# Reordered opening and closing steps of a folded mixture-and-adapter kernel

## Chip, cores and metric

One NeuronCore of a Trainium2 chip runs the whole program as one launch. The metric is the device time of one execution in microseconds (us); lower is better. TensorE (PE) multiplies, VectorE (DVE) and ScalarE (ACT) do the elementwise work and read PSUM, GpSimd (POOL) does elementwise work in SBUF, and SyncE (SP) issues nearly all transfers.

## What is computed

The input x is 64 tiles of 128 rows by 1024 (128 samples of 64 channels). Two layers follow each other; cut to what matters:

```python
c   = einsum('bct,bcd->bdt', x, W[condition])           # channel mix, per sample
q   = c @ Wq.T;  scores = router(q)/sqrt(48) + log_rel  # 256 slots, top 8
w   = softmax over the top 8 of (q . keys)/8 + log_rel
aux = (w @ values) @ Wvd.T @ Wvu.T
u   = clip(0.5*log1p(var)/mean(log1p(var)) + 2.5*sigmoid(gelu(c@Wu1.T+bu1)@Wu2.T+bu2), 0, 5)
x   = x + c + gate(u) * aux
y   = x @ base_weight.T + base_bias + (x @ A[id].T) @ B[id].T   # low-rank adapter
x   = x + base(y) + 0.5 * inverse_fourier(decoded(y))
```

Everything after x in the second layer is linear, so the weights are folded into one 1024 x 1024 matrix M and the adapters into rows of two tables. The mean of log1p(var) runs over all rows, so all 64 tiles must have been seen once before the gate of the first can be computed.

## The kernel before

There are three stages. `setup_stage` and `fold_stage` (to about 276 us of the profiled execution) build M while the variance of every tile is taken. `main_stage` then splits M and small tables into high and low parts and runs the tiles.

M is not used as it is: seven half-size products per tile pair (blocks B11, T1, B21, T2, T3, T4, B22; the named sums T3, T4, B22 are formed on POOL by `t_sums`) give the product of two tiles. Every block is held as two 16-bit parts in two halves, so there are 14 units in the order of `UNITS` (B11, T2, B21, T3, T1, T4, B22). `m_high(u)` on ACT makes the high part (L1197), `m_low(u)` on DVE the low part (L1731). PE waits for a unit before its first use (`product_unit`, L1560).

The main stage is a software pipeline written out by hand as `step(n, q)` on each engine: steps 0 to 3, a loop over 56 steps, then steps 60 to 66. In step n, PE does for tile n the narrow product (8 chunks, L1634), the mix (L1684), and half of the seven products of a pair (an odd step `product_first`, an even one `product_second`); between its chunks stand, for tile n-1, the transposes and the small products of the gate (`aux`, `aux_t`, `adapter`); and for tile n-3 twelve matmuls (L1665 and L1676) that write the output into `out_ps`, from where ACT copies it (L1269) and SP stores it (L1072). Each engine executes its list in order, so a step's wait holds back all that stands behind it there. Order is set by these lists and by semaphores, nothing else.

What stands around the change, by line:

- Opening on DVE: L1780 to L1811, ending in the router's operand (L1803 to L1811, seven instructions that read `score_ps` and the keys and end in `router_split`). Behind it in step 0: the low part of the narrow product `pa_lo` (L1865), which PE needs for the mix; `wa_low`, `row_constants` (with two memsets, L1824); the query (L1892), `variance_norm` (L1830), m_low(2) and (3).
- Step 0 on PE: mix, a matmul for the mean over all rows into `score_ps` (L1692, which waits for `router_split`), the value operand (L1495, whose table `av_t` SP loads at L1103), transpose of the query, scores.
- Step 1 on PE: `aux_t` waits for `u_sb` of DVE (L1854, L1857), itself behind the gate's small steps (L1987 to L1993) and, in step 0, behind m_low(4) and m_low(5). On ACT `split_x(2, 2)` (L1282) and m_high(8) stand behind p1 (L1279); on DVE m_low(8) (L1943) stands before gelu (L1946), lsum (L1949) and u2 (L1957), for which PE waits before the T3 units.
- End of step 2: ACT copies V, the folded value matrix in `out_ps`, to `rhs_a` (L1344); DVE makes its low part twice (`v_low`, L1828, once for each slot of `rhs_b`), then raises `vb_ready`.
- SP before its loop: loads of tiles 4 and 5, then a wait for `vb_ready`, then the adapter rows of tiles 0 and 1 (`load_adapters`, L1117 to L1123).
- Tail: step 65 makes the output of tile 62 (slot 0 of `pm_hi`, `pm_lo`), step 66 that of tile 63 (slot 1), both in `out_ps`. In `last_quarter` the last sum of slot 0 (`u2`, L1849) is taken after the last product; slot 1 is complete before.

## Time and profile before

| | us |
|---|---|
| median of 3 runs (lowest to highest) | 1505.54 (1505.38 to 1508.84) |
| the profiled execution, own time | 1507.83 |
| its span, first to last instruction | 1505.8 |
| PE busy | 1447.3 (96%) |
| DVE busy | 970.4 (64%) |
| ACT busy | 882.6 (59%) |
| POOL busy | 695.1 (46%) |

The page of the profile gives the busy time of each engine, the span in 40 slices with the clock that TensorE was granted, the chain of work that ended last, and the costliest groups. The trace behind it can be asked for what each engine waited for, for the order of instructions in a stretch, and for the busy time by stretch. Lines (L86) are lines of the kernel; L86, L87 and L88 are the three matmuls of every split product.

### The profile page before, as it was taken

The page shows a single profiled execution, that of the slowest core. Times are in us where ns is not written, and L with a number is a line of the kernel's source. Part 1 is how long each engine was busy: PE and PEld are TensorE (multiplying, and loading weights), DVE is VectorE, ACT ScalarE, POOL GpSimd, SP SyncE. Part 2 cuts the span into 40 slices and gives each one's busy share as a digit, 9 for nine tenths or more (in the row PEclk, how much of TensorE's full clock was granted, in tenths as well). Part 3 has the DMA queues.
Part 4 walks back from the last instruction along what each step waited for, and adds up shares of the span by engine and source line. Part 5 has one row for each costly group of instructions (what it writes and reads, how often), then busy time and mean ns, then how long its engine had stood idle before and what let it go on. Part 6 is the DMA issues. An engine that isn't in the chain of part 4 may idle for free.

```text
span 1505.8 us, 28751 instructions
## 1 busy us (share of the span) xinstructions
PE 1447.3 (96%) x7300; PEld 904.2 (60%) x7300; DVE 970.4 (64%) x2744; ACT 882.6 (59%) x1841; POOL 695.1 (46%) x539
## 2 busy tenths in 40 slices
PE   6899999977899999999999999999999999999997
PEld 3677777553555656665555556666555555656664
DVE  6767888887466666666666666566666666666663
ACT  4667666645456555665566555566555556555652
POOL 4756666555444444444444444444444444444440
PEclk9999999979899999999999999999999999999999
DMA  9687665240333333333333333223333333333322
GB/s 309 228 276 257 195 186 171 75 108 5 102 95 93 103 99 100 101 101 95 93 93 96 101 105 92 92 92 92 92 99 103 95 93 93 101 101 99 110 59 77
DMA packets 160951, 176.14 MB, mean 117 GB/s; under 512 B 104851, under 2 KB 123238, under 8 KB 160785
## 3 DMA queue, kind: packets, MB, share of 16 engines
q1 hardware_dynamic: 156118, 161.56, 34.9%
q10 hardware_dynamic: 4795, 14.15, 2.8%
q8 instruction: 15, 0.25, 0.1%
q14 instruction: 23, 0.19, 0.0%
HBM read 135.97 MB, written 39.32 MB: 116 GB/s over the span
## 4 chain that ended last, share of the span: by engine, by line
PE 78%; POOL 7%; issue 6%; DVE 5%; SPq 2%; DMA 1%; ACT 1%; POOLq 0%; ACTq 0%; DVEq 0%
PE pair L86 20%; PE pair L88 19%; PE pair L87 19%; PE pair L1676 7%; POOL v_lo L256 6%; PE pair L1665 6%; PE pair L1507 2%; PE pair L1552 1%; PE pair L1546 1%; PE pair L1545 1%; DVE m_lo L1736 1%; DMA w_kinds<-w_kinds_sb 1%; PE pair L1526 1%; PE pair L1513 0%; SPq L351 0%
## 5 line engine op out<-in xcount | busy, mean ns | idle before, releaser
L1375 POOL TENSOR_TENSOR t_narrow<-t_a_raw,t_narrow 128x256 f16<-128x256 f32 x64 | 42.9, 671 | 574.6 <-ACT x_hi L1189 574.6
L86 PE MATMUL pair<-m_hi,s_hi 128*128 128x512 f16 x512 | 195.6, 382 | 7.8 <-DVE t_u L1957 5.4
L256 POOL TENSOR_TENSOR v_lo<-v_x,v_hi 128x1024 fp32r<-128x1024 f32 x64 | 156.1, 2442 | 91.5 <-ACT v_hi L250 91.4
L87 PE MATMUL pair<-m_lo,s_hi 128*128 128x512 f16 x512 | 194.6, 380 | 0.0
L88 PE MATMUL pair<-m_hi,s_lo 128*128 128x512 f16 x512 | 194.6, 380 | 0.0
L1398 POOL TENSOR_TENSOR s_lo<-t_xt,s_hi 128x512 f16<-128x512 f32 x128 | 145.4, 1166 | 60.6 <-ACT s_hi L1195 60.6
L86 PE MATMUL pair<-t_narrow,x_hi 128*128 128x352 f16 x512 | 161.3, 315 | 1.0 <-DVE t_narrow L1793 1.0
L87 PE MATMUL pair<-t_narrow,x_hi 128*128 128x352 f16 x512 | 161.1, 315 | 0.0
L88 PE MATMUL pair<-t_narrow,x_lo 128*128 128x352 f16 x512 | 161.0, 314 | 0.0
L1377 POOL TENSOR_TENSOR x_lo<-t_xt,x_hi 128x512 f16<-128x512 f32 x128 | 152.0, 1208 | 0.0
L86 PE MATMUL pair<-m_hi,x_hi 128*128 128x512 f16 x384 | 147.5, 384 | 0.3 <-DVE u L1916 0.3
L87 PE MATMUL pair<-m_lo,x_hi 128*128 128x512 f16 x384 | 146.6, 382 | 0.0
L88 PE MATMUL pair<-m_hi,x_lo 128*128 128x512 f16 x384 | 146.5, 382 | 0.0
L1865 DVE SCALAR_TENSOR_TENSOR t_pa_lo<-pair,t_unscale,t_pa_hi 128x320 fp32r<-128x320 f32 (+1 forms) x128 | 45.4, 396 | 121.4 <-ACT t_pa_hi L1256 121.4
L1909 DVE SCALAR_TENSOR_TENSOR t_arg<-t_z 128x256 f32<-128x256 f32 x64 | 58.1, 908 | 85.0 <-ACT t_z L1275 85.0
L247 ACT ACTIVATE squares<-v_x 128x1024 bf16<-128x1024 f32 x64 | 67.4, 1054 | 49.5 <-DVE blk_lo L807 32.7
L1251 ACT CAST t_lhs_a<-pair 128x128 fp32r<-128x128 f32 x64 | 17.0, 266 | 135.4 <-PE pair L1513 135.4
L1295 ACT ACTIVATE t_probs<-t_logits,t_col 128x256 f32<-128x256 f32 x64 | 32.4, 507 | 108.0 <-DVE t_col L1940 108.0
L86 PEld LDWEIGHTS pair<-m_hi,s_hi 128*128 128x128 f16 x512 | 50.0, 98 | 75.6 <-DVE t_u L1957 21.9
L88 PEld LDWEIGHTS pair<-m_hi,s_lo 128*128 128x128 f16 x512 | 50.2, 98 | 60.7 <-issue 0.6
L1185 ACT ACTIVATE t_xt<-t_xt,t_scale 128x512 f32<-128x512 f32 x128 | 84.9, 714 | 0.0
L1269 ACT COPY t_out_sb<-pair 128x1024 f32<-128x1024 f32 x64 | 64.6, 1009 | 28.7 <-PE pair L1676 28.7
(291 smaller groups left out, 3695.2 us busy)
## 6 DMA issues: line engine op xcount, KB each, us to landing
v_x<-in_x SPq DMA_DIRECT2D x64, 512.0 KB, 3.4
t_xt<-in_x_t SPq DMA_DIRECT2D x64, 512.0 KB, 3.2
out<-t_out_sb SPq DMA_DIRECT2D x64, 512.0 KB, 2.7
rhs_b<-bk_hi SPq DMA_DIRECT2D x256, 64.0 KB, 2.3
t_a_raw<-in_lora_a SPq DMA_DIRECT2D x128, 64.0 KB, 2.8
t_bd<-w_kinds SPq DMA_DIRECT2D x128, 64.0 KB, 2.2
t_rhs_c<-bk_lo SPq DMA_DIRECT2D x128, 64.0 KB, 2.2
blk_raw<-in_left_blocks ACTq DMA_DIRECT2D x10, 512.0 KB, 4.7
```

Source lines behind the costliest of these rows:

```text
L86: pe.matmul(out, a_hi, b_hi, start=start, stop=False, skip_group_check=skip)
L87: pe.matmul(out, a_hi, b_lo, start=False, stop=False, skip_group_check=skip)
L88: return pe.matmul(out, a_lo, b_hi, start=False, stop=stop, skip_group_check=skip)
L247: act.activation(v["squares"][:, s, :], v["v_x"][:, slot, :], ACT.Square, accum_out=g["x_sq"][:, bass.ds(n, 1)])
L256: pool.tensor_tensor(v["v_lo"][:, s, :], v["v_x"][:, slot, :], f(v["v_hi"][:, s, :]), ALU.subtract).then_inc(v["v_lo_ready"], 1)
L1185: last = act.activation(rows, rows, ACT.Identity, scale=x_scale(i, half))
L1269: act.copy(b["out_sb"][:, o, :], out_ps[:]).then_inc(s["out_ready"], 1)
L1377: last = pool.tensor_tensor(x16[q][1][:, cols], b["xt"][:, p, cols], x16[q][0][:, cols], ALU.subtract)
L1398: last = pool.tensor_tensor(s16[q // 2][1][:, slot, cols], b["xt"][:, slot, cols], s16[q // 2][0][:, slot, cols], ALU.subtract)
L1665: pe.matmul(out_ps[:, c], lhs, rhs[o][:, c], start=begin, stop=False)
L1676: last = pe.matmul(out_ps[:, c], lhs, rhs[:, c], start=False, stop=end)
L1909: dve.scalar_tensor_tensor(b["arg"][:], b["z2"][:], 1.0, b["z"][:], ALU.add, ALU.mult).then_inc(s["arg_ready"], 1)
```

## The change

It touches no loop iteration; all of it is in the opening steps 0 to 3 and the last two steps.

1. DVE, opening: the constant row's low part (L1784) goes behind the low parts of Wu and Wq; the two memsets go ahead of `a_low(3)`; the router's operand becomes `router_low()` and goes behind z in step 0. The mean's matmul writes the product's bank `pm_ps` and waits for `const_placed`, not for `router_split`.
2. M's low parts on DVE: m_low(5) from the end of step 0 to behind `pa_lo` of step 1; 6 behind z, 7 behind u2, 8 behind the gate of step 1.
3. ACT: an early one-element Tanh in step 0; `sums_high(0, 0)` behind z2 of step 0; the gate's Tanh ahead of e_t in step 0; `split_x(2, 2)` ahead of the query's copy in step 1.
4. V: ACT's copy behind tanh of step 2 (with waits for M's unit and POOL's sum), one `v_low` behind m_low(13), the second slot by a DVE copy in step 3 behind `pa_lo`; PE waits for it before the units of step 3.
5. SP: the adapter rows of tiles 0 and 1 wait for M's low parts, not for V, and go ahead of the loads of tiles 4 and 5.
6. Tail: step 65 makes tile 63, step 66 tile 62, the latter in `pair[2]`; ACT copies its left half, DVE its right half; SP stores in that order.
7. Three SBUF tiles change places.

```diff
-        def store(j, p):
+        def store(j, p, ready=None):
             off = sp.snap(j * (P * HID)) if not isinstance(j, int) else j * P * HID
-            ready = sp.snap(j + 1) if not isinstance(j, int) else j + 1
+            if ready is None:
+                ready = sp.snap(j + 1) if not isinstance(j, int) else j + 1
             sp.wait_ge(s["out_ready"], ready)
             sp.dma_start(bass.AP(t["out"].tensor, off, [[HID, P], [1, HID]]), b["out_sb"][:, p, :]
...
-        load_x(5, 1)
-        sp.wait_ge(s["vb_ready"], 1)
+        sp.wait_ge(s["m16_lo_ready"], len(UNITS))
         sp.wait_ge(s["const_cleared"], 1)
         sp.wait_ge(f_["bk_stored"], 32 * LBLK)
         load_adapters(0, 0)
         load_adapters(1, 1)
+        load_x(4, 0)
+        load_x(5, 1)
...
+            if isinstance(n, int) and n == NT + 3:
+                sp.wait_ge(s["half_ready"], 1)
+            if isinstance(n, int) and n > NT + 1:
+                store(old_tile(n - 1), 1 - p, n - 3)
+            else:
+                store(n - 4, p)
...
+
+    def old_tile(n):
+
+        return 2 * NT - n if isinstance(n, int) and n > NT else n - 3
+
+    def old_slot(n, q):
+        return old_tile(n) % 2 if isinstance(n, int) else 1 - q % 2
+
+    def last_one(n):
+        return isinstance(n, int) and n == NT + 2
...
-            o = 1 - p
+            o = old_slot(n, q)
...
+                act.activation(col[0:1, 15:16], g["ones"][0:1, 0:1], ACT.Tanh)
+            if isinstance(n, int) and n == 1:
+                act.wait_ge(s["wa_stored"], 16)
+            if p == 1 and (not isinstance(n, int) or n + 2 < NT):
                 split_x(n + 1, (q + 1) % 4)
...
             if has_old(n):
                 act.wait_ge(s["out_done"], n - 2)
-                act.wait_ge(moved[o], arrived(n - 3, o, 16))
-                act.copy(b["out_sb"][:, o, :], out_ps[:]).then_inc(s["out_ready"], 1)
+                act.wait_ge(moved[o], arrived(old_tile(n), o, 16))
+                if last_one(n):
+                    act.copy(b["out_sb"][:, o, LEFT], pair[2][:, LEFT]).then_inc(s["out_ready"], 1)
+                else:
+                    act.copy(b["out_sb"][:, o, :], out_ps[:]).then_inc(s["out_ready"], 1)
...
+            if isinstance(n, int) and n == 0:
+                act.wait_ge(s["wa_mm_done"], KC // 2)
+                sums_high(0, 0)
...
             if isinstance(n, int) and n == 1:
-                act.wait_ge(s["wa_stored"], 16)
-                split_x(2, 2)
...
+            if isinstance(n, int) and n == 2:
+                act.wait_ge(s["m16_lo_ready"], m_units(T1, 2))
+                act.wait_ge(s["t_ready"], 2 * SUMMED.index(B22) + 2)
+                act.wait_ge(s["v_mm_ready"], 2)
+                act.copy(b["rhs_a"][:], out_ps[:]).then_inc(s["va_ready"], 1)
...
+            start = isinstance(n, int) and n == 0
+            if start:
+                gate_tanh()
             if has_new(n):
                 act.wait_ge(s["et_done"], n + 1)
                 act.copy(b["e_t"][:].rearrange("p c n -> p (c n)"), misc_ps[:, P:3 * P]
                          ).then_inc(s["et_ready"], 1)
-                act.wait_ge(s["unorm_ready"], n + 1)
-                act.activation(c1(GTANH), c1(UNORM), ACT.Tanh, scale=b["gates"][:, 4:5],
-                               bias=b["gates"][:, 5:6]).then_inc(s["gtanh_ready"], 1)
+            if has_new(n) and not start:
+                gate_tanh()
...
-                act.wait_ge(s["m16_lo_ready"], len(UNITS))
-                act.wait_ge(s["v_mm_ready"], 2)
-                act.copy(b["rhs_a"][:], out_ps[:]).then_inc(s["va_ready"], 1)
...
+            o = old_slot(n, q)
+            oq = old_tile(n) % 4 if isinstance(n, int) else (q - 3) % 4
+            bank = pair[2] if last_one(n) else out_ps
...
-                if p:
-                    pe.wait_ge(s["c_lo_ready"], n * 2 - 2)
-                if not isinstance(n, int) or n > 3:
+                if last_one(n):
+                    pe.wait_ge(s["c_lo_ready"], NT * 2)
+                elif p:
+                    pe.wait_ge(s["c_lo_ready"], NT * 2 - 2 if isinstance(n, int) and n > NT else n * 2 - 2)
+                if last_one(n):
+                    pe.wait_ge(s["pa_lo_ready"], NT)
+                    pe.wait_ge(s["z_ready"], NT)
...
-                pe.wait_ge(s["h_ready"], n - 2)
-                pe.wait_ge(loaded["lora"][o], arrived(n - 3, o, LPT))
+                pe.wait_ge(s["h_ready"], old_tile(n) + 1)
+                pe.wait_ge(loaded["lora"][o], arrived(old_tile(n), o, LPT))
...
                 pe.wait_ge(s["lsum1_ready"], 1)
-                pe.wait_ge(s["router_split"], 2)
-                pe.matmul(score_ps[:, 0:1], g["ones"][:], b["mean"][:, 0:1], start=True, stop=True
+                pe.wait_ge(s["const_placed"], 1)
+                pe.matmul(pm_ps[:, 0:1], g["ones"][:], b["mean"][:, 0:1], start=True, stop=True
                           ).then_inc(s["mean_done"], 1)
...
+            if isinstance(n, int) and n == 3:
+                pe.wait_ge(s["vb_ready"], 2)
...
+        dve.memset(f(b["q_b"][BOT:P, :]), 1.0)
+        dve.memset(f(b["lhs_c"][:]), 1.0)
...
-        dve.wait_ge(s["const_hi_ready"], 1)
-        dve.tensor_tensor(b["rhs_c"][BOT:BOT + 1, 0, :], pm_ps[BOT:BOT + 1, :], f(b["rhs_c"][BOT:BOT + 1, 0, :]),
-                          ALU.subtract).then_inc(s["const_placed"], 1)
...
+        dve.wait_ge(s["const_hi_ready"], 1)
+        dve.tensor_tensor(b["rhs_c"][BOT:BOT + 1, 0, :], pm_ps[BOT:BOT + 1, :], f(b["rhs_c"][BOT:BOT + 1, 0, :]),
+                          ALU.subtract).then_inc(s["const_placed"], 1)
...
-        dve.wait_ge(s["router_mm_done"], 2)
...
+        def router_low():
+            dve.wait_ge(s["router_mm_done"], 2)
+            dve.tensor_scalar(router[0][:], score_ps[:, 2 * BOT:2 * BOT + NSLOT], float(RDIM) ** -0.5, None, ALU.mult)
+            link(dve.tensor_scalar(router[1][:], keys, float(BOT) ** -0.5, None, ALU.mult))
...
-            dve.memset(f(b["q_b"][BOT:P, :]), 1.0)
-            dve.memset(f(b["lhs_c"][:]), 1.0)
...
-            link(dve.tensor_scalar(b["mean"][:, 1:2], score_ps[:, 0:1], 1.0 / (NT * P), 1e-6, ALU.mult, ALU.add))
+            link(dve.tensor_scalar(b["mean"][:, 1:2], pm_ps[:, 0:1], 1.0 / (NT * P), 1e-6, ALU.mult, ALU.add))
...
+            if last_one(n):
+                dve.wait_ge(s["out_done"], NT)
+                dve.wait_ge(moved[0], arrived(old_tile(n), 0, 16))
+                dve.tensor_copy(b["out_sb"][:, 0, RIGHT], pair[2][:, RIGHT]).then_inc(s["half_ready"], 1)
...
+            if isinstance(n, int) and n == 3:
+                dve.wait_ge(s["vb_ready"], 1)
+                dve.tensor_copy(b["rhs_b"][0:BOT, 1, :], f(b["rhs_b"][0:BOT, 0, :])).then_inc(s["vb_ready"], 1)
...
             if one:
-                m_low(6)
+                m_low(5)
...
             if start:
+                router_low()
                 variance_norm()
                 m_low(2)
                 m_low(3)
             if one:
-                m_low(7)
+                m_low(6)
...
+                dve.wait_ge(s["m16_lo_ready"], len(UNITS))
+                dve.wait_ge(s["va_ready"], 1)
+                v_low(0).then_inc(s["vb_ready"], 1)
...
-            if one:
-                m_low(8)
...
+            if one:
+                m_low(7)
...
-            if start:
-                m_low(5)
...
+            if one:
+                m_low(8)
...
-            if isinstance(n, int) and n == 2:
-                dve.wait_ge(s["va_ready"], 1)
-                v_low(0)
-                v_low(1).then_inc(s["vb_ready"], 1)
```

## Rows read from the trace of the kernel before

**Rows 1.** Stretch, length; busy PE, PEld, DVE, ACT, POOL; granted clock; DMA share, GB/s.

```profile
421.40:439.40 18.00, 17.96 (x97) 10.57 (x96) 10.15 (x35) 11.91 (x27) 9.62 (x9) 1.00 0.35 110
...
312.00:321.70 9.70, 9.70 (x43) 8.65 (x44) 9.12 (x29) 4.41 (x10) 0.00 (x0) 0.50 0.39 59
329.30:335.50 6.20, 6.18 (x19) 3.05 (x20) 4.93 (x10) 0.74 (x3) 3.70 (x2) 0.50 0.43 119
347.20:352.50 5.30, 5.29 (x16) 2.54 (x17) 2.96 (x8) 3.95 (x7) 5.22 (x5) 0.50 0.01 3
377.80:389.90 12.10, 9.32 (x27) 6.24 (x28) 3.26 (x10) 5.39 (x11) 2.89 (x3) 0.50 0.43 127
...
1494.30:1497.50 3.20, 3.06 (x12) 2.18 (x12) 0.00 (x0) 0.07 (x1) 0.00 (x0) 1.00 0.00 0
```

**Rows 2.** What TensorE waited for, 255 to 420 us: total, times, longest.

```profile
PE pair L1513 <- DVE t_u_sb L1857: 5.8, 2, 3.9
PE pair L86 <- DVE t_u L1957: 5.4, 1, 5.4
PE pair L86 <- DVE t_pa_lo L1865: 3.7, 1, 3.7
PE pair L86 <- issue: 2.8, 2, 1.9
PE pair L1676 <- DMA t_rhs_c<-bk_lo: 2.8, 1, 2.8
PE pair L86 <- DVE c L1929: 1.1, 1, 1.1
PE pair L86 <- DVE t_narrow L1793: 1.0, 1, 1.0
```

**Rows 3.** VectorE in order of time: start, duration, line, operation, idleness before.

```profile
305.03 0.41 DVE L1803 TENSOR_SCALAR t_gelu<-pair 128x256 f32<-128x256 f32 x1
...
308.94 1.48 DVE L1809 TENSOR_TENSOR t_router_b<-t_penalty,t_router_a 64x256 fp32r<-64x256 f32 x1
...
321.96 2.22 DVE L1736 SCALAR_TENSOR_TENSOR m_lo<-m,t_scale,m_hi 128x1024 f16<-128x1024 f32 x1
...
340.90 1.86 DVE L1736 SCALAR_TENSOR_TENSOR m_lo<-m,t_scale,m_hi 128x1024 f16<-128x1024 f32 x1 [1.05 <-ACT m_hi L1203]
...
344.09 2.45 DVE L1949 CUSTOM_DVE_ANT_0 t_z<-t_gelu,t_wu 128x256 f32<-128x256 f32 x1
...
374.29 2.35 DVE L1828 TENSOR_TENSOR rhs_b<-pair,rhs_a 64x1024 fp32r<-64x1024 f32 x2 [2.03 <-ACT rhs_a L1344]
```

**Rows 4.** ScalarE in order of time, opening.

```profile
336.70 0.51 ACT L1182 ACTIVATE t_a_raw<-t_a_raw,t_scale 128x256 f32<-128x256 f32 x1
...
339.72 1.15 ACT L1203 ACTIVATE m_hi<-m,t_scale 128x1024 f16<-128x1024 f32 x1
...
373.27 1.00 ACT L1344 CAST rhs_a<-pair 128x1024 fp32r<-128x1024 f32 x1
```

**Rows 5.** GpSimd in order of time: the two B22 sums of t_sums.

```profile
343.74 5.00 POOL L1370 TENSOR_TENSOR m<-m 128x1024 f32<-128x1024 f32 x2
```

**Rows 6.** SyncE: the value table's issue and landing; the fifth tile's load.

```profile
L1103 SPq DMA_DIRECT2D t_out_sb<-in_av_t x1: 427/427/427, 305.3 to 305.3; - x1
...
DMA to landing us min/median/max: 5.7/5.7/5.7
...
374.85 0.35 SPq L1018 DMA_DIRECT2D t_xt<-in_x_t  x1
```

**Rows 7.** The tail in order of time: VectorE, TensorE twice, ScalarE.

```profile
1490.87 0.75 DVE L1841 SCALAR_TENSOR_TENSOR pm_lo<-u,t_unscale,pm_hi 128x512 fp32r<-128x512 f32 x1 [0.22 <-ACT pm_hi L1331]
...
1494.34 0.73 PE L1665 MATMUL pair<-t_pm_hi,t_bd 128*128 128x512 f32 x2 [2.48 <-DVE t_pm_lo L1841]
...
1498.50 0.73 PE L1665 MATMUL pair<-pm_hi,t_bd 128*128 128x512 f32 x2 [1.10 <-ACT t_out_sb L1269]
...
1501.60 1.01 ACT L1269 COPY t_out_sb<-pair 128x1024 f32<-128x1024 f32 x1 [3.15 <-PE pair L1676]
```

38 lines of the change are left out of this document (17 added, 21 removed).

## Prediction, made before the changed kernel was built or run

> **What bounds the kernel now.** I read the busy times by stretch first. In a steady step of 18.0 us TensorE is busy 17.96 [rows 1]: nothing that another engine does can shorten the loop, and the change leaves its iterations alone. So I looked for the stretches where TensorE is not full, or not at full clock. There are two: the opening steps, about 302 to 400 us, and the last 14 us. For the opening I read what TensorE waited for: seven entries, from 1.0 to 5.8 us, sum 22.7 us [rows 2]. In the same stretch the granted clock was 0.50, the lower level (1.2 GHz), four times, each begun after or amid such waits; in three of them (from 329.3, 347.2 and 377.8) TensorE worked 6.18, 5.29 and 9.32 us at half speed [rows 1], so they cost about 3.1, 2.6 and 4.7 us more. That is the fund the opening can give back. The tail has a wait of 2.5 us for the last low part and one of 1.1 us for ScalarE's copy of the only output bank [rows 7].
>
> **The change, part by part.**
>
> *Before the mix of step 0 (items 1 and 3).* The constant row moves behind the low parts of Wu and Wq, so the wait of 1.0 us for them [rows 2] goes. `router_low` took from 305.03 to 308.94 + 1.48, so 5.4 us [rows 3], and stood ahead of the `pa_lo` for which TensorE waited 3.7 us [rows 2]; it now stands behind z, and that wait goes too. But 4.7 us aren't gained. Next on TensorE is the value operand, whose table is issued at 305.3 and lands 5.7 us later, at 311.0 [rows 6]; SyncE's list up to it is unchanged, and TensorE began that work at about 312.0 (where the stretch of busy, half-clock work begins in [rows 1]). The floor is thus 311.0, and behind it the scores still wait for `router_low` and `norm_ready`: on VectorE the same work comes before them as before, less two memsets that now stand in its idle time. I take 1.0 us, between 0 and 3.5 (less contention in `router_low` and a shorter half-clock stretch). The early Tanh only brings the table load into ScalarE's idle time, where TensorE sits waiting anyway: nothing.
>
> *aux_t of step 1 (items 2 and 3).* Ahead of the gate's small steps stood m_low(5), 2.22 us [rows 3], and on ScalarE e_t; both now stand behind. TensorE's two waits for u_sb are 5.8 in all, the longer 3.9 [rows 2], so this one is 1.9; it goes whole. m_low(5) comes behind `pa_lo`, in place of m_low(6), so nothing new stands there. The next wait, `pa_lo` of step 1 ("issue", 1.9, [rows 2]), hangs on the same chain from the transpose through ScalarE and stays.
>
> *u2 of step 1 (items 2 and 3), the largest.* TensorE waited 5.4 us [rows 2]. On VectorE m_low(8) ran from 340.90 for 1.86 us, having waited for ScalarE's high part, then gelu, then lsum, 2.45 us, up to 346.5 [rows 3]; ScalarE had first to do `split_x(2, 2)` and m_high(8), from 336.70 to 339.72 + 1.15 [rows 4]. The split now runs at the start of the step, while TensorE does the mix, so tanh comes at about p1 plus 1.1 us; m_low(8) is gone from ahead of gelu. What stays is contention: m_low(8) ended at 342.8 and gelu at 344.1, 1.3 us, and lsum took 2.45, both for 256 columns where m_low(5) needed 2.22 for 1024 [rows 3]. Meanwhile GpSimd was forming the B22 sums, 2.5 us each [rows 5], and in the new order those sums fall there again. I count 2.3 us of wait left, so 3.1 gained (bounds 0.4 to 5.4).
>
> A rule speaks against this part. VectorE's lsum took 2.45 us beside GpSimd's sums of 2.5 us each. The Trainium skill, SBUF — State Buffer, section "Who interferes with whom", says that a VectorE instruction with two SBUF inputs and a GpSimd instruction that reads SBUF take the shared port as an exclusive lock, and the later one blocks until the first ends. By that rule gelu and lsum could each wait out a whole sum, and the gain here would fall by 2.7 us, to 0.4; the trace agrees in kind, with one of the two (lsum) near such a full wait.
>
> *Query of step 1.* At full clock TensorE reaches the transposition before q is split; I charge 0.7, between nothing and the 1.1 us of the nearest row, the wait for c22 [rows 2].
>
> *m_low(7) and (8)* now stand behind u2 and behind the gate. Behind u2 the T3 units of step 1 need only unit 6, and 7 is needed a narrow product later. m_low(8) stands ahead of `u_sb` of step 2: 1.2 to 1.86 us, covered partly by five narrow chunks; I charge 1.0 (0 to 1.9).
>
> *V (item 4).* Before: ScalarE's copy at 373.27, 1.00 us [rows 4], and two low parts of 1.2 each, from 374.29 [rows 3], kept u2 and u_sb of step 3 back: the wait of 3.9 us [rows 2]. Now one of them, 1.2 us, stands in step 2 behind m_low(13). Behind it on VectorE queue top8 and the sum c22, for which TensorE already waited 1.1 us [rows 2]: that wait grows by 1.2. The 3.9 goes whole, since the gate and u2 then end before TensorE's seventh chunk of step 3. Its new waits for POOL's sum (ended at 348.7, [rows 5]) and for M's unit are long met. The copy of the second slot stands ahead of the adapter's low part, but TensorE passes `vb_ready` only after twelve output matmuls: nothing. If that cover failed, it would cost at most another 1.2 us.
>
> *Adapter rows (item 5).* TensorE waited 2.8 us for them [rows 2], issued after four loads and V. With those ahead of them gone they are issued in step 2: 2.8 gained. The price is on the queue: the fifth tile's load (374.85, [rows 6]) stays bound by POOL's low sums, which slide by V's 1.2 us, while step 3's units come earlier by what is freed ahead of them (3.9 + 2.8 + 4.7, less 1.2). `split_x(4)`, 3.0 us as in [rows 4], then stands on ScalarE ahead of the output copy and the query of step 3, and the scores and the exponential wait: I charge 1.8 (0 to 4).
>
> *Clock.* If the waits go, the half-clock stretches that followed them go: 3.1 + 2.6 + 4.7 = 10.4. One row bears on whether the waits that stay (1.9, 2.3) are harmless: in the tail a wait of 2.5 us was followed by a stretch at 1.00 [rows 1, 7]. I take 10.4; kept, they would cost up to all of it.
>
> *Tail (item 6).* Slot 1 is complete at 1490.87 + 0.75 = 1491.6 [rows 7], just as the products end, so tile 63 runs at once, 3.06 us [rows 1], to 1494.8. Tile 62's low part was ready for 1494.34 [rows 7]: it starts without a wait and ends at 1497.9, against 1501.6. The last copy is shared by two engines: 1.01 [rows 7] to an estimated 0.6, half and a start. The last store starts 4.2 us earlier; the store before it will be 2.7 us old by then. Bounds 3.3 to 4.3.
>
> *SBUF places:* nothing.
>
> **Sum.** Opening gains 1.0 + 1.9 + 3.1 + 3.9 + 2.8 + 10.4 = 23.1; charges 0.7 + 1.0 + 1.2 + 1.8 = 4.7; net 18.4. With the tail 22.6. The profiled execution has 1507.8 around a span of 1505.8, so a span of 1483.2 and an own time of 1485.2; the median of the runs was 2.3 below that execution, so 1482.9, said as **1483**.
>
> **The rivals.**
>
> *The clock stays low.* What is left is a chain of shorter waits (1.9, 0.7, 2.3, 1.0), and before the lower level began at 329.3 after two waits of only 1.9 each. Two stretches stay whole and the third by half: 3.1 + 2.6 + 2.3 = 8.0 less gain, 1491. For it: those two waits; against it: the tail. 0.22.
>
> *The port decides.* All of VectorE's two-input steps beside GpSimd go as the lsum did: 2.7 more at u2, 1.9 in m_low and the gate: 4.6 less gain, 1487.5. The Trainium skill's rule named above is this mechanism. 0.12.
>
> *More is freed.* Contention misses gelu and lsum, and tile 4 arrives in time: 2.3 + 1.8 + 1.0 plus 1.5 of the first half-clock stretch, 6.6 more gain, 1476. 0.12.
>
> *Only the tail.* The opening would be bound by transfers: ScalarE's `split_x(2, 2)` now stands ahead of query, z2, p1, tanh and exp, and its tile waits on SyncE for the round trip of the split table. If it landed 18 us later than I count, the opening gives nothing: 1501, within what a measurement can't tell from no change. 0.06.
>
> *Slower.* V's new place waits on a chain that crosses three engines: v_low on VectorE, for ScalarE's copy, for GpSimd's second B22 sum. Every us by which that sum ends after m_low(13) holds back top8, c22, the B22 units and u_sb. It ended at 348.7 [rows 5]; v_low is due some 17 us after it (an estimate: the old place, 374.29 [rows 3], less the eight or so us of step 2 that it moves ahead of). The kernel turns slower by over 4.5 us only if GpSimd lagged by 17 + 22.6 + 4.5 = 44 us; a lag of 50 gives 1516. Against it: GpSimd's work in the stretch isn't larger. 0.04.
>
> The forecast itself has 0.44, with a range of its own of 1479 to 1487. The range of 1474 to 1494 takes in the first four cases and leaves out the last two. A measurement here tells about 0.3% (4.5 us) from no change: faster 0.90, same 0.06, slower 0.04.
>
> **What would show it.** In the profile after: no wait of TensorE for t_narrow, for `t_pa_lo` of step 0, for `t_u_sb`, nor for the adapter's transfer; the value operand at 311.0, not before; the wait for u2 about 2 us; that for c22 over 2; granted clock 1.00 from about 322 on; the start of step 4's narrow product some 18 us earlier; in the tail, twelve matmuls right after the products and twelve more right behind. The prediction is wrong if the clock table still shows 0.50 after 322, or if SyncE's loads of tiles 2 and 4 come late.

## The result and the profile after

The changed kernel took 1489.83 us (median of 4 runs, 1487.25 to 1493.16) beside 1505.57 for the kernel before: a ratio of 0.9892, interval 0.9868 to 0.9916, or 15.7 us less. The forecast was 1483 with a range of 1474 to 1494: the sign and the range held, the size fell short by 6.8 us. The narrower range that the forecast gave to its own case, 1479 to 1487, did not hold. The profiled execution has 1487.25 around a span of 1485.2, the shortest of the four, while the one of before was 2.3 us above its median. So the two profiles differ by 20.6, and the medians by 15.7; both are used below, and it is said which.

What TensorE waited for, 255 to 420 us, changed kernel (total, times, longest), to be read against [rows 2]:

```profile
PE pair L86 <- DVE t_u L2006: 3.3, 1, 3.3
PE pair L86 <- issue: 2.8, 2, 1.9
PE pair L86 <- DVE c L1980: 2.1, 1, 2.1
PE pair L86 <- DVE vd L2014: 1.4, 1, 1.4
PE pair L1542 <- DVE t_u_sb L1897: 1.3, 2, 0.8
PE pair L1524 <- DMA t_out_sb<-in_av_t: 1.2, 1, 1.2
PE pair L86 <- DVE t_pa_lo L1909: 1.2, 1, 1.2
PE pair L1701 <- DVE t_pm_lo L1881: 1.0, 1, 1.0
PE pair L86 <- DVE t_narrow L1830: 0.8, 1, 0.8
PE pair L1574 <- ACT t_q_b L1295: 0.6, 1, 0.6
```

The waits for the adapter rows (2.8) and for u_sb of step 3 (3.9) are gone, and the others of [rows 2] are shorter, but for the two "issue" waits, which stay, and the one for c22, which grew by 1.0. In their place stand waits for `vd` (1.4) and for a low part in step 3 (1.0) that the prediction doesn't name, and one for the value table (1.2), which it names as the floor. The granted clock in the same stretch (stretch, length, PE busy, clock, DMA share, GB/s), to be read against [rows 1]:

```profile
308.00:311.00 3.00, 2.45 (x12) 0.51 0.82 131
311.00:314.00 3.00, 3.00 (x14) 0.50 0.44 69
314.00:318.00 4.00, 4.00 (x19) 0.50 0.09 8
318.00:336.00 18.00, 13.96 (x74) 0.99 0.34 91
336.00:339.00 3.00, 0.09 (x1) 0.97 0.01 3
339.00:342.00 3.00, 2.61 (x8) 0.50 0.03 5
342.00:349.00 7.00, 5.35 (x36) 0.98 0.00 0
349.00:352.00 3.00, 2.81 (x8) 0.51 0.12 11
372.00:384.00 12.00, 11.39 (x57) 1.00 0.38 104
```

Of the four stretches at 0.50 in [rows 1] the first is as long as it was (308 to 318), the second and the longest, in step 3, are gone (372 to 384 is at 1.00), and in place of the third there are two of some 3 us, behind the waits for u2 (339 to 342) and for u_sb (349 to 352).

The tail is as worked out. The twelve output matmuls of tile 63 follow the products, tile 62's follow without a gap, and the last copy is shared. TensorE, ScalarE and VectorE of the changed kernel in order of time (start, duration, engine, line, operation), to be read against [rows 7]:

```profile
1475.52 0.73 PE L1701 MATMUL pair<-pm_hi,t_bd 128*128 128x512 f32 x2
...
1478.42 0.64 PE L1701 MATMUL pair<-t_pm_hi,t_bd 128*128 128x512 f32 x2
...
1481.42 0.59 ACT L1289 COPY t_out_sb<-pair 128x512 f32<-128x512 f32 x1 [1.79 <-PE pair L1712]
...
1481.42 0.69 DVE L1905 COPY t_out_sb<-pair 128x512 f32<-128x512 f32 x1 [3.30 <-PE pair L1712]
```

Step 4's first output matmul starts at 387.34, against 403.56 before. Of these 16.2 us, 2.0 were there before 300 already, ahead of all that the change touches (the same matmul of the fold starts at 286.62 and started at 288.61). So by the profiles the opening gave 14.2 and the tail 4.4, the part of the 20.6 that comes behind step 4's first output matmul.

### The profile page after: what moved, and what is told of

It reads as the page before. It is cut to its first block, busy times and chain, and to the rows that moved or that the text cites. A ratio compares the mean times of both kernels' runs of the same rounds, so it can differ in the third digit from the quotient of the medians.

```text
span 1485.2 us, 28758 instructions
## 1 busy us (share of the span) xinstructions
PE 1439.8 (97%) x7300; PEld 900.8 (61%) x7300; DVE 970.4 (65%) x2745; ACT 882.3 (59%) x1842; POOL 703.3 (47%) x539
## 4 chain that ended last, share of the span: by engine, by line
PE 79%; POOL 7%; DVE 6%; issue 6%; ACT 1%; DMA 1%; SPq 0%; POOLq 0%; ACTq 0%; DVEq 0%
PE pair L86 20%; PE pair L88 19%; PE pair L87 19%; PE pair L1712 7%; POOL v_lo L256 7%; PE pair L1701 6%; PE pair L1536 2%; PE pair L1574 1%; PE pair L1575 1%; PE pair L1581 1%; DVE m_lo L1774 1%; PE pair L1555 1%; PE pair L472 1%; DMA fourier<-in_fourier 1%; PE pair L1542 1%
## 5 line engine op out<-in xcount | busy, mean ns | idle before, releaser
L256 POOL TENSOR_TENSOR v_lo<-v_x,v_hi 128x1024 fp32r<-128x1024 f32 x64 | 159.5, 2497 | 86.7 <-ACT v_hi L250 86.5
L250 ACT CAST v_hi<-v_x 128x1024 fp32r<-128x1024 f32 x64 | 66.7, 1042 | 23.4 <-PE pair L88 23.3
```

The source lines that it names most:

```text
L250: act.copy(v["v_hi"][:, s, :], v["v_x"][:, slot, :]).then_inc(v["v_hi_ready"], 1)
L256: pool.tensor_tensor(v["v_lo"][:, s, :], v["v_x"][:, slot, :], f(v["v_hi"][:, s, :]), ALU.subtract).then_inc(v["v_lo_ready"], 1)
```

## The experiments

All are edits of the changed kernel unless said otherwise. Each kernel was timed beside the kernel before on its own chip; "R" is that ratio with its interval. Differences between experiments are differences of R times 1506 us, with the mean of the two ratios of the changed kernel, 0.9900, as the base. The interval of one ratio reaches some 3 us to either side and that of a difference of two some 4 us, so a difference under 4 us is only a hint.

**The changed kernel once more.**

> The changed kernel once more, nothing edited. It shows how much of what TensorE does after its waits in steps 1 and 2 differs from run to run. Every theory expects 1487 to 1493 us and the same waits within 0.3 us (u2 of step 1 about 3.3, c22 2.1, vd 1.4, u_sb of step 2 0.85, pm_lo 1.0). Theory 'the clock's low level varies': the stretches at 0.50 after the u2 wait and after the u_sb wait (2.6 and 3.5 us in the first profile) change in length or vanish in one of the profiles, and the span changes by half of that. Rival: they are the same in both profiles, to 0.3 us, and the spread of 6 us between runs comes from elsewhere.

1491.54 us (1488.48 to 1493.63), R 0.9908, 0.9887 to 0.9928. Same waits within 0.1 us for u2, c22, vd and u_sb, and the stretches at 0.50 behind them again 3 to 4 us each (340 to 345, 351 to 355). The theory falls: the low level does not differ from run to run in steps 1 and 2. It does differ in step 0, where it lasted from 308.1 to 318.3 in the first profile and from 313.4 to 320.3 in this one. What differs besides is where the opening starts. TensorE's first narrow product, ahead of any of its waits that the change touches but one, in the first profile of the changed kernel (start, duration, line, idle time before it and what ended that):

```profile
300.17 0.32 PE L86 MATMUL pair<-t_narrow,x_hi 128*128 128x352 f16 x1 [0.84 <-DVE t_narrow L1830]
```

And in the second:

```profile
302.88 0.31 PE L86 MATMUL pair<-t_narrow,x_hi 128*128 128x352 f16 x1 [1.47 <-POOL x_lo L1406]
```

Over all profiles of this study this start lies between 300.2 and 304.0. Of the 2.7 us between these two, 2.3 are still there when the value operand starts (308.55 and 310.81) and 1.2 at step 4, behind the shorter stretch at the low level; the spans differ by 1.2 too. The runs without a profile reach up to 6 us above the profiled one, and what they lose it in can't be seen.

**The tail alone**, on the kernel before: item 6 of the change, nothing else.

```diff
+                if last_one(n):
+                    act.copy(b["out_sb"][:, o, LEFT], pair[2][:, LEFT]).then_inc(s["out_ready"], 1)
...
-            o, oq = 1 - p, (q - 3) % 4
+            o = old_slot(n, q)
+            oq = old_tile(n) % 4 if isinstance(n, int) else (q - 3) % 4
+            bank = pair[2] if last_one(n) else out_ps
```

> The kernel before, with the new order of the last two output tiles alone (half copies, second bank and stores included), the opening as it was. If tail and opening add up as I worked them out, it takes 1501.3 us (4.2 less than before, bounds 3.3 to 4.3), and its opening shows the old waits (u_sb 5.8, t_u 5.4, V 3.9). Rival, by which the opening alone moved the time and the tail's saving is lost in the last store: 1505.5. Rival in which the shortfall of the whole is in the tail: under 3 us of gain.

1501.21 us, R 0.9965, 0.9953 to 0.9976: 5.3 us by the ratio, 4.9 by the medians. Forecast 4.2. Its opening shows the old waits (u2 5.4, u_sb 4.9, adapter rows 2.6). From step 4's first output matmul to the end its profile has 1097.8 us, as that of the changed kernel has (1097.9), against 1102.2 before: 4.4. Nothing of the shortfall is in the tail.

**V and the adapter rows back.** ScalarE's copy goes from behind tanh to the end of step 2 (not shown), the low parts and the rows as here:

```diff
-                v_low(0).then_inc(s["vb_ready"], 1)
...
-                dve.tensor_copy(b["rhs_b"][0:BOT, 1, :], f(b["rhs_b"][0:BOT, 0, :])).then_inc(s["vb_ready"], 1)
...
+                v_low(0)
+                v_low(1).then_inc(s["vb_ready"], 1)
...
-        load_adapters(0, 0)
-        load_adapters(1, 1)
         load_x(4, 0)
         load_x(5, 1)
+        sp.wait_ge(s["vb_ready"], 1)
+        load_adapters(0, 0)
+        load_adapters(1, 1)
```

> The changed kernel with V and the adapter rows back at their old places: ScalarE's copy and both low parts at the end of step 2, the adapter rows behind V and behind the loads of tiles 4 and 5. By my sum it is slower than the changed kernel by 3.9 (wait for V) + 2.8 (adapter rows) + 4.7 (half clock after them) - 1.2 (V's low part ahead of c22) - 1.8 (charge for tile 4's split) = 8.4 us, so 1498. If the clock had nothing to do with it, by 3.7 us, 1493.5. If these two waits had been hidden behind ScalarE's chain (which stands before both in step 3), by under 1.5 us.

1497.98 us, R 0.9944, 0.9923 to 0.9965: 6.6 us slower than the changed kernel, between the two sums. What its TensorE waited for:

```profile
PE pair L1540 <- DVE t_u_sb L1893: 4.3, 2, 3.9
...
PE pair L1710 <- DMA t_rhs_c<-bk_lo: 2.7, 1, 2.7
```

Its clock (stretch, length, PE busy, granted clock, DMA share, GB/s):

```profile
371.00:374.00 3.00, 2.02 (x6) 0.50 0.70 209
374.00:382.00 8.00, 5.27 (x16) 0.50 0.45 139
382.00:385.00 3.00, 3.00 (x10) 0.56 0.09 25
```

Both waits are back with their old lengths (3.9 and 2.7), and 9.9 us of matmul work run at 0.50 behind them, 5 us lost. In return the wait for c22 is 1.1 instead of 2.1, as I charged, and the wait of 1.0 for a low part in step 3 is gone. From the first narrow product to step 4's first output matmul this profile has 95.3 us, against 87.2 and 85.7 in the two of the changed kernel, so 8.1 to 9.6 more. The ratio shows less, and both sums (8.4 and 3.7) lie within its uncertainty of some 4 us, so it doesn't tell by itself what share the clock has.

**GpSimd's B22 sums made small.** 16 of 256 columns are summed; the other columns of the block stay unsummed, so this leaves out part of the computation.

```diff
-                    pool.tensor_tensor(out, t2, m_block(T1, j), ALU.add).then_inc(s["t_ready"], 1)
+                    pool.tensor_tensor(out[:, :, 0:16], t2[:, :, 0:16], m_block(T1, j)[:, :, 0:16], ALU.add
+                                       ).then_inc(s["t_ready"], 1)
```

> The changed kernel, but GpSimd forms only 16 of the 256 columns of each B22 sum (the rest of the block is left out of the product, so the output isn't the reference's). GpSimd then doesn't work beside VectorE's gelu, lsum and m_low(7) in step 1. Theory 'the shared port': gelu and lsum (1.93 and 2.45 us beside the sums) fall to 0.4 to 0.5 us each, u2 starts about 3 us earlier, TensorE's wait for it (3.3) falls under 0.5, the low level of the clock behind it goes, and the kernel takes 3.3 + 1.3 = 4.6 us less, 1485. Rival 'they wait for something else' (tanh, the accumulator): the two keep their times and nothing moves, 1490. Rival 'ScalarE's chain is the bound': gelu and lsum are short, but the wait for u2 stays above 2 us.

1486.93 us, R 0.9870, 0.9851 to 0.9889: 4.5 us less. VectorE in step 1 of the changed kernel (start, duration, line, operation):

```profile
334.31 1.93 DVE L1995 SCALAR_TENSOR_TENSOR t_gelu<-t_th,t_z 128x256 f32<-128x256 f32 x1
336.27 2.45 DVE L1998 CUSTOM_DVE_ANT_0 t_z<-t_gelu,t_wu 128x256 f32<-128x256 f32 x1
...
339.25 2.19 DVE L1774 SCALAR_TENSOR_TENSOR m_lo<-m,t_scale,m_hi 128x1024 f16<-128x1024 f32 x1
```

GpSimd's two B22 sums in the same profile, in one row:

```profile
333.56 4.88 POOL L1399 TENSOR_TENSOR m<-m 128x1024 f32<-128x1024 f32 x2
```

And the same VectorE instructions in the kernel with small sums:

```profile
340.30 0.42 DVE L1996 SCALAR_TENSOR_TENSOR t_gelu<-t_th,t_z 128x256 f32<-128x256 f32 x1
340.75 0.42 DVE L1999 CUSTOM_DVE_ANT_0 t_z<-t_gelu,t_wu 128x256 f32<-128x256 f32 x1
...
341.71 1.27 DVE L1775 SCALAR_TENSOR_TENSOR m_lo<-m,t_scale,m_hi 128x1024 f16<-128x1024 f32 x1
```

Beside the sums gelu took 1.93, lsum 2.45 and M's part 7 2.19 us; without them 0.42, 0.42 and 1.27. The wait for u2 is gone from the list, and so is that for u_sb of step 2. In the changed kernel gelu ends 0.2 us after the first sum (half of 4.88, so at 336.0) and lsum 0.2 to 0.3 us after the second (338.44): each waited out what was left of a sum. The whole is less clear than these rows. TensorE's transposes of u_sb in steps 1 and 2 start 23.0 us apart in the changed kernel (they are shown below, with u2 first) and 18.8 apart here, so this stretch gave 4.2. But the profiled run, with 1489.68, is the longest of its four, and its span is no shorter than the changed kernel's: the low level of the clock lasted from 312 to 329 around step 0, some 7 us longer than in the first profile of the changed kernel, and two more stretches at that level stand at 332 to 336 and 363 to 367, each a little longer than those at 339 and 349. The 4.5 us rest on the ratio, and on the stretch of 18.8. That gelu and lsum each waited out a sum is what the rule of the Trainium skill says that the prediction names (SBUF — State Buffer, "Who interferes with whom"), and the trace agrees with it for both.

**M's low parts back in their old order**: 5 at the end of step 0, 6 behind `pa_lo`, 7 behind z, 8 ahead of gelu.

```diff
+            if start:
+                m_low(5)
...
             if one:
-                m_low(5)
+                m_low(6)
...
+            if one:
+                m_low(8)
             if has_new(n):
                 dve.wait_ge(s["tanh_ready"], n + 1)
```

> The changed kernel with M's low parts on VectorE back in their old order (unit 5 at the end of step 0, 6 behind pa_lo, 7 behind z, 8 ahead of gelu); ScalarE keeps its new order, with tile 2's split early. Theory 'the low parts on VectorE are what freed TensorE': the wait for u_sb of step 1 grows from 0.4 by 1.3 to 1.9, the wait for u2 from 3.3 by 1.9 to 2.3 (unit 8 beside GpSimd's sums), the wait for u_sb of step 2 (0.85) goes in return, and the clock costs 0 to 2 more: 3 to 5 us slower than the changed kernel, 1494.5 to 1496.5. Rival 'ScalarE's earlier split did it': under 1 us slower, and the wait for u2 stays at 3.3.

1495.22 us, R 0.9932, 0.9912 to 0.9952: 4.8 us slower. Two waits of its TensorE grew as the expectation says, both a little more:

```profile
PE pair L86 <- DVE t_u L2008: 5.7, 1, 5.7
...
PE pair L1542 <- DVE t_u_sb L1897: 2.4, 1, 2.4
```

**The router's operand back ahead of step 0.**

```diff
+        router_low()
+
         def wa_low():
...
-                router_low()
                 variance_norm()
```

> The changed kernel with the router's operand back ahead of step 0. By my prediction that part is worth 1.0 us at most net, since behind the mix TensorE waits for the value operand's table anyway (landed at 308.5 in the changed kernel): 1490 to 1492.5, no more than 1 us slower. Rival 'the queue of VectorE decides': the operand takes 2.2 us where it is now, beside no work of GpSimd, and 5.4 us in its old place; the mix starts 4 us later, TensorE's next work then starts at about 312.5 instead of 308.6, and all is 3 to 4 us later: 1494 to 1495.5.

1489.84 us, R 0.9894, 0.9874 to 0.9914: no difference (0.9 less, inside the interval). TensorE waits 2.0 us for `pa_lo` of step 0 instead of 0.3 (in the second profile of the changed kernel) and then not at all for the value table instead of 1.7: the mix starts 2.5 us later (310.8 against 308.3), 0.8 of which is the later start of the first narrow product, and the value operand only 0.9 (311.7 against 310.8). This floor was the prediction's reason for counting 1.0 instead of 4.7, and even the 1.0 can't be found in the time.

**u2 of step 1 ahead of gelu.**

```diff
+            if one:
+                dve.wait_ge(s["prod_done"], n * 4 - 2)
+                dve.wait_ge(s["p1_ready"], n + 1)
+                dve.tensor_tensor(u2[:], pm_ps[:, RIGHT], p1[:], ALU.add).then_inc(s["sums_done"], 1)
             if has_new(n):
                 dve.wait_ge(s["tanh_ready"], n + 1)
...
-            if first_part(n, q):
+            if first_part(n, q) and not one:
```

> The changed kernel with one move: in step 1 VectorE forms the sum u2 ahead of gelu and lsum instead of behind them. Theory 'the wait only moves': u2 is in time for TensorE, so its wait of 3.3 goes, but gelu, lsum and the gate end when they did, and TensorE arrives 3.3 us earlier at u_sb of step 2: that wait grows from 0.85 to about 4, and the kernel gains under 1 us (1490 to 1491.5). Rival 'the wait is worth its length': 3.3 us and the half-clock stretch behind it (1.3 us) go, 1486.5 to 1488.

1491.18 us, R 0.9901, 0.9884 to 0.9918: nothing gained. Its wait for u2 is 0.2, and at the head of its list stands:

```profile
PE pair L1542 <- DVE t_u_sb L1897: 3.5, 1, 3.5
```

The wait has moved to u_sb of step 2, as its expectation says. The transposes for which TensorE waits for u_sb, of steps 1 and 2, in the changed kernel (start, duration, in brackets the idle time and what ended it):

```profile
323.80 0.33 PE L1542 MATMUL pair<-ident,t_u_sb 128*128 128x128 f32 x1 [0.41 <-DVE t_u_sb L1897]
346.82 0.33 PE L1542 MATMUL pair<-ident,t_u_sb 128*128 128x128 f32 x1 [0.85 <-DVE t_u_sb L1897]
```

And with u2 first:

```profile
326.63 0.27 PE L1542 MATMUL pair<-ident,t_u_sb 128*128 128x128 f32 x1
349.57 0.33 PE L1542 MATMUL pair<-ident,t_u_sb 128*128 128x128 f32 x1 [3.46 <-DVE t_u_sb L1897]
```

They are 23.0 and 22.9 us apart. In the second profile of the changed kernel and in that with the router's operand back it is 23.0 as well. TensorE's longest wait wasn't what held this stretch; the chain up to u_sb on VectorE was.

**A combined version**: u2 first, GpSimd's B22 sums behind tile 3's split, M's part 8 behind u_sb of step 2 and part 4 behind u_sb of step 1, V's low part behind c22.

```diff
+            if one:
+                m_low(4)
+            if isinstance(n, int) and n == 2:
+                m_low(8)
...
-                if isinstance(n, int) and n == 1:
-                    t_sums(B22)
                 split_x(n + 2, (q + 2) % 4)
+                if isinstance(n, int) and n == 1:
+                    t_sums(B22)
```

> The changed kernel with what its waits ask for, all together: u2 of step 1 ahead of gelu; GpSimd's B22 sums behind tile 3's split, so that they don't run beside gelu and lsum; M's low part 8 behind u_sb of step 2 and part 4 behind u_sb of step 1, where VectorE was idle 1.6 and 1.5 us; V's low part behind the sum c22. From the rows of the changed kernel: wait for u2 3.3 and its half-clock stretch 1.3 gone, vd 1.4 to 0.2, c22 2.1 to 0.9, less 0.5 that u_sb of step 2 may still wait: 6.7 us less, 1484.5. Rival 'the port follows': the B22 sums now run beside M's parts 7 to 9 and VectorE's queue ends no earlier: the wait for c22 or for T3's low part (unit 7) grows by 2 to 3 us and the gain is under 3 us. Rival 'the clock': the waits shrink, but stretches at 0.50 come elsewhere, and the gain is 3 to 5 us.

1487.76 us (1487.42 to 1489.34), R 0.9879, 0.9862 to 0.9896: 3.2 us less than the changed kernel, a hint by the intervals, and half of the 6.7 that its expectation has. gelu and lsum took 0.42 and 0.43 and TensorE doesn't wait for u2, but the sums now stand beside the gate. The two transposes of u_sb are 20.2 us apart, 2.8 less than in the changed kernel. Its VectorE there:

```profile
341.25 0.90 DVE L2045 SCALAR_TENSOR_TENSOR t_col<-t_col 128x1 f32<-128x1 f32 x1
342.19 2.28 DVE L2049 TENSOR_TENSOR t_col<-t_col 128x1 f32<-128x1 f32 x1
```

And its GpSimd, the two sums in one row:

```profile
342.08 4.67 POOL L1399 TENSOR_TENSOR m<-m 128x1024 f32<-128x1024 f32 x2
```

A product of one element per partition (0.16 us elsewhere) took 2.28 us: it began 0.1 us after the first sum did and ended about when that did (half of 4.67 from 342.08 is 344.4).

**Matmuls that nobody reads in TensorE's waits**, to keep it busy:

```diff
+        def junk(q, dst, times):
+            for _ in range(times):
+                pe.matmul(dst, x16[q][0][:, 0:P], x16[q][0][:, 0:HALF], start=True, stop=True)
...
+                if start:
+                    pe.wait_ge(s["const_placed"], 1)
+                    junk(q, pm_ps[:, RIGHT], 4)
+                if one:
+                    pe.wait_ge(s["logits_ready"], 1)
+                    junk(q, score_ps, 8)
```

> The changed kernel with matmuls that nobody reads (128x128 by 128x512, f16, 0.216 us each at full clock as the products' rows show) in TensorE's longest waits: 4 ahead of the mix of step 0, 7 ahead of the value operand, 8 ahead of the mix of step 1, 14 ahead of the wait for u2, 3 ahead of the transpose and 4 ahead of the mix of step 2. Nothing else changes. Theory 'the idle time brings the low clock': TensorE arrives at each wait's end as before, the stretches at 0.50 after 339 and after 349 don't come, and the one from about 310 shrinks: 3.0 us less for the two (half of 2.8 and 3.2 us of busy time at 0.50), up to 6 with the first: 1485 to 1488. Rival 'the low clock isn't from the waits': same stretches, same time or up to 1 us more, 1490 to 1492.5.

1489.20 us (1487.02 to 1490.01), R 0.9885, 0.9864 to 0.9906: 2.3 us less by the ratio, a hint, and 0.1 by the profiles (387.2 against 387.3 at step 4, with the first narrow product at 300.2 in both). Its clock (columns as above):

```profile
336.00:339.00 3.00, 3.00 (x15) 1.00 0.01 3
339.00:342.00 3.00, 2.72 (x16) 1.00 0.00 0
342.00:349.00 7.00, 5.36 (x37) 1.00 0.00 0
349.00:352.00 3.00, 2.95 (x14) 1.00 0.12 11
```

Both stretches at 0.50 are gone: they came from the idle time before them. But the time that TensorE saved came back as waits for VectorE (u_sb of step 2 from 0.8 to 1.6, c22 from 2.1 to 2.3), and the two transposes of u_sb are 23.0 us apart as before. The first stretch came from 313.1 to 323.4, 5 us later than in the first profile of the changed kernel and as long. But in the second one, with nothing filled, it came at 313.4 too, so that its place can't be put down to the filling.

**Tile 2's split back behind p1** on ScalarE.

```diff
-            if p == 1 and (not isinstance(n, int) or n + 2 < NT):
+            if p == 1 and (not isinstance(n, int) or 1 < n < NT - 2):
                 split_x(n + 1, (q + 1) % 4)
...
             if isinstance(n, int) and n == 1:
+                act.wait_ge(s["wa_stored"], 16)
+                split_x(2, 2)
                 m_high(8)
```

> The changed kernel with ScalarE's split of tile 2 back behind p1 in step 1, ahead of unit 8's high part and of tanh. The split is 3.1 us on ScalarE. Theory 'ScalarE's chain holds u2': tanh comes 3.1 us later (about 335.5 instead of 332.1), gelu waits for it 1.2 us instead of following the logits at 334.3, and GpSimd's split and B22 sums start 3 to 5 us later, so that they still run beside lsum: the wait for u2 grows from 3.3 to 4.5 to 6, 1491.5 to 1494. Rival: GpSimd's sums move off gelu and lsum, which fall to 0.4 each, the wait for u2 stays at 3.3 or below and nothing is lost: 1489 to 1491.

1490.17 us, R 0.9896, 0.9872 to 0.9919: no difference. The rival holds for the time, not for the 0.4 us: gelu waited 1.33 for tanh but took 0.75, lsum 1.26, and the wait for u2 was 2.1. What ScalarE loses, VectorE gets back, since GpSimd's sums come 5 us later too.

**The combined version with unread matmuls in its waits**: the two edits above joined, with these counts changed.

```diff
-                    junk(q, score_ps, 3)
+                    junk(q, score_ps, 6)
...
-                    junk(q, score_ps, 4)
+                    junk(q, score_ps, 8)
...
-                for _ in range(14):
+                for _ in range(2):
```

> The combined version with the same unread matmuls in the waits that it has left: 4 and 7 in step 0, 8 ahead of the mix of step 1, 2 ahead of T3's units, 6 ahead of the transpose and 8 ahead of the mix of step 2. In its profile 5.1 us of busy time lay at 0.50 after the wait of 1.6 and that of 2.1 in step 2, and 10.0 us from 312 on. Theory 'the idle time brings the low clock': 2.5 us less, up to 7.5 with the first stretch, 1480.5 to 1485. Rival: unchanged, 1487 to 1489.

1486.31 us (1485.92 to 1486.96), R 0.9864, 0.9843 to 0.9885: 5.4 us less than the changed kernel, and 2.3 less than the combined one (1.5 by the medians). No run of the one is as long as any of the other, but they ran on different chips and the intervals of their ratios overlap, so this gain is a hint. It is the lowest ratio of all. The low clock behind step 2's waits is gone; in step 0 it is still there, at 315 to 318 and 321 to 325.

**Three more moves in VectorE's queue** (part 5 of M behind z, 11 behind u3, 13 behind c22), on that version.

```diff
                 m_low(10)
-                m_low(11)
...
                 dve.tensor_tensor(u3[:], pm_ps[:, RIGHT], p1[:], ALU.add).then_inc(s["sums_done"], 1)
+                if isinstance(n, int) and n == 2:
+                    m_low(11)
...
-                m_low(13)
...
                 dve.tensor_tensor(c22[:], pm_ps[:, LEFT], u3[:], ALU.add).then_inc(s["sums_done"], 1)
+            if isinstance(n, int) and n == 2:
+                m_low(13)
```

> The combined and filled version with three more moves in VectorE's queue: M's part 5 from ahead of the query of step 1 to behind z, part 11 of step 2 behind the sum u3, part 13 behind the sum c22. In the combined and filled version's rows TensorE waits 0.8 us for the query of step 1, 1.8 for u3, 1.1 for c22, with parts of M of 1.9, 4.0 (two) and 2.5 us (two) ahead of them. Theory 'the order of VectorE's queue is what is left': the query comes 1.9 us earlier, u3 2.0 and c22 1.2 us earlier; the waits for u3 and c22 go to under 0.3 each and 2.5 to 3 us are gained: 1483.5 to 1484. Rival 'only its length counts': the same work comes before u_sb of step 3 and each wait taken away comes back at the next one: 1486 to 1487. Rival 'GpSimd follows': T4's second sum waits for part 5, comes 2 us later and delays tile 2's split and the narrow product of step 2: 1487 to 1489.

1491.32 us, R 0.9891, 0.9874 to 0.9907: 4 us slower, at the edge of what can be told. TensorE's instructions behind its waits in step 2 (start, duration, in brackets the idle time and what ended it), in the version without these moves:

```profile
355.98 0.39 PE L86 MATMUL pair<-m_hi,x_hi 128*128 128x512 f16 x1 [1.82 <-DVE u L1987]
359.83 0.39 PE L86 MATMUL pair<-m_hi,s_hi 128*128 128x512 f16 x1 [1.09 <-DVE c L2000]
362.44 0.44 PE L1581 MATMUL pair<-ident,t_probs 128*128 128x128 f32 x2 [0.49 <-ACT t_probs L1323]
```

And with them:

```profile
355.01 0.39 PE L86 MATMUL pair<-m_hi,x_hi 128*128 128x512 f16 x1 [0.69 <-DVE u L1985]
358.87 0.39 PE L86 MATMUL pair<-m_hi,s_hi 128*128 128x512 f16 x1 [1.09 <-DVE c L1999]
362.80 0.44 PE L1581 MATMUL pair<-ident,t_probs 128*128 128x128 f32 x2 [1.81 <-ACT t_probs L1323]
```

u3 and c22 come 1 us sooner, and the exponential, behind part 13, V's low part and the logits, 0.4 later. The waits come back at the next point, as the first rival says. The other rival, "GpSimd follows", came true as well, one step earlier: TensorE was 1.2 us ahead at the transpose of u_sb of step 1 (323.74 against 324.94) and no longer at that of step 2 (344.56 against 344.39). T4's second sum on GpSimd started at 330.2 instead of 329.0 and took 3.3 us instead of 2.4, and beside it VectorE's step ahead of tanh took 2.59 instead of 0.89. From the value operand to step 4 that makes 2.1 us more (79.0 against 76.9). The profiles don't show the whole 4 us, though, and the clock of its slower runs is as high (0.996 to 0.998) as that of its fastest: where they lose 4 us is open.

## Why the prediction was right and where not

By parts, forecast and as measured by undoing or isolating each:

| part | forecast | measured |
|---|---|---|
| tail | 4.2 | 5.3 |
| V and adapter rows, with clock and charges | 3.9 + 2.8 + 4.7 - 1.2 - 1.8 = 8.4 | 6.6 |
| M's low parts, split and query, with clock and charges | 1.9 + 3.1 + 3.1 + 2.6 - 0.7 - 1.0 = 9.0 | 4.8 (order) - 0.6 (split) = 4.2 |
| router, constant row | 1.0 | -0.9 |
| sum | 22.6 | 15.2 (whole: 15.1) |

Each measured part carries up to some 4 us of uncertainty, the tail 2. That they add up to 0.1 us is luck; it shows only that no large part is missing. The largest share of the shortfall stands in the third row, and that this is so is no more certain than its numbers.

**The step that failed: the clock's term was added to the waits' (10.4 us).** The mechanism is right: TensorE filled through its waits kept 1.00 in steps 1 and 2, and with V's waits back 9.9 us ran at 0.50 again. In step 3 the term was worth 5.0 us by these rows, where I had counted 4.7; the ratio doesn't separate it from the waits. In steps 1 and 2 it failed twice. The waits that stayed brought the low level back (2.6 and 2.8 us of busy time at 0.50 behind u2 and u_sb; with shorter waits before, 318 to 336 stayed at 0.99). And even where the level was kept up, the profile gained 0.1 us, since TensorE then waited longer for VectorE. I had worked as if TensorE's rate set the end of these steps. The distance of the two transposes of u_sb says otherwise: 23.0 us with the waits, 22.9 with the wait for u2 taken away, 23.0 with TensorE at full clock throughout. The busy times fit that. The changed kernel between the same two points (stretch, length, then PE, PEld, DVE, ACT and POOL busy, clock, DMA share, GB/s):

```profile
323.70:346.80 23.10, 16.69 (x81) 8.53 (x81) 20.32 (x36) 15.28 (x31) 19.36 (x12) 0.93 0.17 43
```

The kernel before:

```profile
327.00:355.00 28.00, 20.59 (x82) 10.42 (x83) 17.35 (x35) 15.09 (x30) 20.87 (x14) 0.76 0.18 51
```

VectorE is busy 20.3 of 23.1 us now (88%) and was busy 17.35 of 28.0 (62%); TensorE has 16.7. The change took the idle time out of VectorE's queue, and the chain through that queue became the bound in this stretch; the experiments with u2 first and with the waits filled show it, since each wait of TensorE that was taken away came back at the next one. The 20.3 us are not all work: with the small B22 sums VectorE is busy 14.8 us between the same points, and the distance is 18.8. Part of the bound is thus time in which VectorE stood behind GpSimd. Of the rivals, "the clock stays low" (1491) is nearest to the result, for half of its reason.

**u2 of step 1.** Forecast: 2.3 us of wait left; measured 3.3, of the 5.4. gelu and lsum each waited out a sum of GpSimd; I had taken one of them so. "The port decides" had the mechanism and its price here (up to 2.7 us of the 3.1) was too high: 1.0 was lost. The small B22 sums show what all of it is worth, 4.2 us in the stretch and 4.5 by the ratio. Its neighbours went the same way: M's parts 2 and 3 took 3.38 us beside GpSimd's low sums (2.47 before, without them) and the step behind them 1.37 instead of 0.42. ScalarE's earlier `sums_high(0, 0)` had moved these sums there, so the copy of `vd` came late and TensorE waited 1.4 us; no run undoes this move by itself. The prediction gives it no price, neither for the instruction nor for what it sets going on GpSimd.

**aux_t of step 1.** Forecast: the wait of 1.9 goes whole; 0.4 is left, and with M's order back it is 2.4, so the order is worth 2.0 of it. Nearly right.

**V and the adapter rows.** Both waits went whole, and the charge on c22 was 1.0 for 1.2. The charge for tile 4 (1.8) was at most 0.6, the wait for `q_b`, and absent in the second profile. The transfer did come late, though: ScalarE waited 4.6 us for it in step 3 (3.4 in the second profile), where the kernel before had no such wait. Not foreseen was 1.0 us for the low part in step 3: TensorE now comes to its output matmuls before VectorE is through with the third low part.

**Router and value operand.** The floor at the table's landing was right, and set the start: TensorE began at 308.55 (312.0 before, with 2.0 of that shift not from the change), and the move by itself measures nothing. I said 311.0; the table was issued 1.9 earlier, at 303.4 (305.5 in the second profile, with the operand at 310.81). The wait of 1.0 ahead of the first narrow product, which the prediction has going whole, stayed: 0.8 in one profile, and 1.5 for GpSimd's low part of x in the other.

**m_low(8) and u_sb of step 2.** Forecast 1.0, measured 0.85, with 2.31 us for the part beside GpSimd.

**Tail.** Right at 4.4 in the profile, for 4.2. The two half copies took 0.59 and 0.69 us, for 0.6.

**From profile to median.** I set the sum against one profiled execution of before and took off its 2.3 above the median. For the changed kernel the profiled run was 2.6 below its median, so the profile shows 20.6 where the medians show 15.7. The two profiles alone would have put the miss at 2.0 us. How near the number comes thus depends on which executions are compared.

**The signs that it named.** "The prediction is wrong if the clock table still shows 0.50 after 322": it does, at 339 to 342 and at 349 to 352, and tile 4's load came late as well. The waits for `t_narrow`, for `t_pa_lo` of step 0 (1.2, and 0.3 in the second profile) and for `t_u_sb` are smaller but not gone. Step 4's narrow product starts 16.2 us earlier, 18 were named. By its own signs the account of the opening was thus wrong in part, though the time lies in the stated range, which took in the rivals too. Two sums in it are off by 0.1: the seven waits make 22.6, and 1491.6 and 3.06 make 1494.7.

## What to carry to other kernels

A wait of the bounding engine is worth its length only if nothing behind it is late as well. Before adding up waits, compare the busy time of the engine that ends them between two of its results with the time between these: at 88% little idle time was left to free here, and what helped was to shorten what is in the queue: 4.2 us of this stretch went when VectorE no longer stood behind GpSimd's sums. A gain in the clock is then in the same pot as the waits, and not on top of them. When an instruction is moved forward, follow what it releases on GpSimd, and look at which two-input VectorE instructions stand there now.

## What was not expected

- Instructions of VectorE from 128x1 to 128x1024 waited out what was left of GpSimd's: 2.28 us for a 128x1 product that took 0.16 elsewhere. GpSimd pays too: its low part of the narrow operand (128x256) took 1.65 us beside VectorE's parts of M and 0.67 without them.
- Unread matmuls in TensorE's waits kept its clock at 1.00 and, on a version whose VectorE queue was eased first, came with a time 2.3 us shorter by the ratios (1.5 by the medians); by the intervals that is a hint.
- The low level in step 0 was not done away with by filling two waits: 10.3 us of it stayed. Its start and length there differ between two profiles of one kernel (10.2 us from 308.1, 6.8 from 313.4), and what sets them is open.
- Runs of one kernel differ by 5 us without a loss in the mean clock (0.996 at 1487.5, 0.998 at 1492.6), and the first narrow product starts anywhere from 300.2 to 303.7 in kernels that do the same work up to there. What brings this is open.
